# Rows and router of two MoE FFNs in wide pieces kept on chip, the shared expert with stationary weights during the routing

## What is computed

```
x = x + 0.5 * ffn(norm(x))
x = x + attention(norm(x))
x = x + 0.5 * ffn(norm(x))        # the same weights again

ffn(x):  scores = sigmoid(x @ gate_w)                      # 16 experts
         selected = top 2 of scores + expert_bias
         w = scores[selected] / (their sum + 1e-20)
         shared = (silu(x @ sg) * (x @ su)) @ sd           # every token
         routed = sum over the two e: w_e * (silu(x @ g_e) * (x @ u_e)) @ d_e
         return shared + routed                            # hidden width 128
attention(x): per head of 3, per batch of 512 rows:
         S = Q K^T / 16; w = softmax(S, over the queries); w V
         mean over the heads, @ fc_w.T + fc_b
```

## Time and profile before

| | us |
|---|---|
| median of 3 executions | 603.43 |
| lowest and highest | 601.87, 606.74 |
| the profiled execution | 605.9 |
| its span, first to last instruction | 604.7 |
| TensorE busy in it | 478.6 (79%) |
| VectorE busy | 366.6 (61%) |
| ScalarE busy | 274.9 (45%) |
| GpSimd busy | 270.1 (45%) |
| mean granted clock of TensorE | 0.918 of full |

### The profile page before, as it was taken

One profiled execution on the slowest core, in us unless ns is written; L12 is line 12 of the kernel. 1 busy time (PEld: TensorE's weight loads), 2 busy tenths in 40 slices (PEclk: granted clock), 3 DMA queues, 4 the chain that ended last, 5 costly groups with the idle time before them and its releaser, 6 DMA issues.

```text
span 604.7 us, 10587 instructions
## 1 busy us (share of the span) xinstructions
PE 478.6 (79%) x3212; PEld 434.0 (72%) x3212; DVE 366.6 (61%) x1118; ACT 274.9 (45%) x771; POOL 270.1 (45%) x278
## 2 busy tenths in 40 slices
PE   3632389999886799799899988999675899999600
PEld 3632389999774598699879977999563799998500
DVE  5567477566566366557645865543637776766543
ACT  3451147677541444354435443456241277776200
POOL 4654536566042163255226522422203566660675
PEclk9999999999998899899989999999955599999755
DMA  8661134667762010011001100010110156677455
GB/s 277 202 210 34 53 106 150 180 189 147 177 199 70 5 48 2 0 36 54 18 1 41 48 19 2 0 36 1 36 61 10 34 149 177 184 164 177 125 159 142
DMA packets 41077, 56.29 MB, mean 93 GB/s; under 512 B 6272, under 2 KB 33792, under 8 KB 41024
## 3 DMA queue, kind: packets, MB, share of 16 engines
q1 hardware_dynamic: 33024, 34.88, 17.8%
q0 software_dynamic: 7584, 20.72, 15.0%
q10 hardware_dynamic: 416, 0.02, 0.0%
HBM read 36.99 MB, written 18.61 MB: 92 GB/s over the span
## 4 chain that ended last, share of the span: by engine, by line
PE 59%; DVE 14%; DMA 12%; issue 5%; ACT 5%; POOL 5%; SPq 0%; POOLq 0%; ACTq 0%; DVEq 0%
PE bank L299 47%; PE bank L305 6%; DMA stage<-y_dram,slot_i 5%; DMA raw<-xn_dram,gather_at 2%; PE bank L432 2%; DMA raw<-xn_dram 2%; DVE x_sb L991 1%; PE bank L334 1%; POOL stage L1217 1%; DVE softmax_row L1114 1%; POOL w_lo L1167 1%; PE bank L389 1%; DVE x_sb L957 1%; DVE xn L817 1%; DMA xn_dram<-xn 1%
## 5 line engine op out<-in xcount | busy, mean ns | idle before, releaser
L299 PE MATMUL bank<-w_hi,xT 128*128 (+1 forms) x504 | 128.6, 317 | 0.0
L1323 POOL TENSOR_TENSOR e_sp<-raw,e_sp 128x512 fp32r<-128x512 f32 x48 | 62.5, 1302 | 134.7 <-ACT e_sp L773 134.6
L1246 POOL DMA_INDIRECT raw<-xn_dram,gather_at x94 | 89.3, 950 | 57.7 <-PE bank L305 46.8
L299 PEld LDWEIGHTS bank<-w_hi,xT 128*128 128x128 f32 x504 | 92.7, 202 | 0.3
L1217 POOL DMA_INDIRECT stage<-y_dram,slot_i x64 | 61.2, 957 | 51.8 <-issue 26.4
L299 PEld LDWEIGHTS bank<-v_sp,e_sp 128*128 128x128 f32 x576 | 75.8, 194 | 4.0 <-POOL e_sp L1323 1.1
L299 PE MATMUL bank<-v_sp,e_sp 128*128 128x256 f32 x576 | 78.0, 286 | 0.9 <-POOL e_sp L1323 0.9
L299 PE MATMUL bank<-g_sp,xT 128*128 128x512 f32 x288 | 75.2, 396 | 1.4 <-DVE g_sp L1022 1.4
L299 PE MATMUL bank<-w_lo,xT 128*128 (+1 forms) x252 | 74.2, 294 | 0.0
L299 PE MATMUL bank<-w_hi,e_sp 128*128 (+1 forms) x252 | 71.3, 303 | 2.0 <-DVE x_sb L1015 1.8
L305 PE MATMUL bank<-ident,raw 128*128 128x128 f32 x292 | 62.4, 298 | 8.8 <-DMA raw<-xn_dram 5.5
(11 more groups left out here) (112 smaller groups left out, 892.1 us busy)
## 6 DMA issues: line engine op xcount, KB each, us to landing
y_dram<-stage SPq DMA_DIRECT2D x94, 128.0 KB
raw<-xn_dram SPq DMA_DIRECT2D x32, 128.0 KB, 2.3
stage<-in_w_pack SPq DMA_DIRECT2D x9, 384.0 KB, 3.5
raw<-in_w_pack SPq DMA_DIRECT2D x8, 384.0 KB, 3.7
xn_dram<-raw SPq DMA_DIRECT2D x20, 128.0 KB, 1.7
x_sb<-in_x SPq DMA_DIRECT2D x4, 512.0 KB, 5.6
out<-x_sb SPq DMA_DIRECT2D x16, 128.0 KB, 2.3
raw<-xn_dram,gather_at POOLq DMA_INDIRECT x94, 3.4
```

The source lines that it names most:

```text
L299: m = pe.matmul(dst, lhs[k][l], rhs[k][r], start=(first and k == 0 and i == 0), stop=(last and k == n - 1 and i == 2), skip_group_check=True)
L1246: pool.indirect_dma_start(row_buf[:, n % ROWS, :], None, xn_dram, bass.IndirectOffsetOnAxis(ap=gather_at[:, j:j + 1], axis=0)).then_inc(s_ ...
L1323: pool.tensor_tensor(e_sp[:, i, 1, :], e32[:, i, :], e_sp[:, i, 0, :].bitcast(F32), ALU.subtract).then_inc(s_e_lo, 1)
```

## The change

Sizes: `STAGES` is 6 instead of 4 (a new buffer `stage_more`). New buffers lie over memory that is free in that stretch: `xn_all` (all 16 normed tiles) and `x_front` over the fold products, `pick_lane` for all 32 pairs and `pick_tile` over `xn_all`.

1. *Norm in wide pieces.* `front_stats` on VectorE and `front_rstd` on GpSimd measure a batch; ScalarE writes normed rows to `xn_all`; one 512 KB DMA stores a batch. In FFN 2 the first three batches still go through `previous_front` and are reloaded by three DMAs of 512 KB near the end of the attention.
2. *Turned rows stay on chip.* Pairs of tiles are turned into one PSUM bank and split into `front_x`, one buffer of 512 columns a batch, with both parts. The router of FFN 1 and of FFN 2's last batch reads these with `three_pass` against a split gate, six matmuls a tile.
3. *Shared expert with stationary weights.* For a batch, the shared weights are the stationary operand and 512 token columns move: 12 matmuls of 512 columns, one silu, one multiply, one copy and one subtraction of 128x512, then 12 matmuls of 256 columns for Y and two additions to `x_sb`. No shared item is left among the items, which are the 47 slot tiles. In FFN 1 batches 0 to 2 run during the routing and batch 3 after the slot tiles; in FFN 2 all four run during the routing.
4. *Slot index without a ring.* All picks have a buffer. VectorE and GpSimd write lanes, VectorE the tile factors of four tiles at a time with two wide instructions, and TensorE runs all 32 matmuls at one place, behind chunks of eight.
5. *Folds* stand at slot steps 12, 24 and 36, and 3 to 5 behind the slot tiles.

```diff
+    CHUNK = 8
+    EARLY_SHARED = 3
-    STAGES = 4
+    STAGES = 6
+    FOLD_STEPS = (12, 24, 36)
...
+            def front_turn(r, n):
...
+                if n >= 2:
+                    pe.wait_ge(s_pair_lo, r * FRONT_PAIRS + n - 1)
...
+                for q in range(2):
+                    for k in range(KH):
+                        m = pe.transpose(bank[n % 2][:, k * PAIR + q * P:k * PAIR + (q + 1) * P],
+                                         xn_all[:, 2 * n + q, k * P:(k + 1) * P], ident[:])
...
+            def front_router(r, n):
...
+                for q in range(2):
...
+                    m = three_pass(logits_all[:, t * E:(t + 1) * E],
+                                   [[x[:, part, k, cols] for part in range(2)] for k in range(KH)],
+                                   [[gate_sp[:, part, k, :] for part in range(2)] for k in range(KH)])
...
+            def shared_gu(r, b):
...
+                if r == 0 and b >= EARLY_SHARED:
+                    pe.wait_ge(s_hT_lo, NI)
+                    pe.wait_ge(s_y_copy, NI)
+                    pe.wait_ge(s_act, NI)
...
+                if r == 1 and b == 1:
+                    pe.wait_ge(s_mix_add, NT)
+                for half, done in ((0, s_sg), (1, s_su)):
...
+                    three_pass(bank[shared_banks(b)[half]][:], lhs, rhs).then_inc(done, 1)
...
+            def shared_y(r, b):
...
+                pe.wait_ge(s_slo, c + 1)
...
+                    m = three_pass(bank[q // 2][:, q % 2 * H:(q % 2 + 1) * H],
+                                   [[shared_hT[:, part, q * P:(q + 1) * P] for part in range(2)]],
+                                   [[w_hi[:, at:at + H], w_lo[:, at:at + H]]])
...
+            def index_tokens(r):
+                chunks = len(pairs_of) // CHUNK
+                for c in range(chunks):
+                    pe.wait_ge(s_lane_dve, r * DVE_LANES + (c + 1) * DVE_LANES // chunks)
+                    pe.wait_ge(s_lane_pool, r * POOL_LANES + (c + 1) * POOL_LANES // chunks)
+                    pe.wait_ge(s_pick_tile, r * chunks + c + 1)
```

```diff
+            for n in range(FRONT_PAIRS + 1):
+                if n < FRONT_PAIRS:
+                    front_turn(0, n)
+                if n > 0:
+                    front_router(0, n - 1)
+            shared_gu(0, 0)
+            shared_gu(0, 1)
+            rank_tokens(0)
+            shared_y(0, 0)
+            shared_gu(0, 2)
+            pack_experts(0)
+            shared_y(0, 1)
+            index_tokens(0)
+            shared_y(0, 2)
...
+            ffn(0, between1)
+
+            shared_gu(0, 3)
+            fold(next(folded))
+            shared_y(0, 3)
+            for n in folded:
+                fold(n)
...
             for w in MIXED_LATER:
+                if w == U - 1:
+                    front_turn(1, 0)
+                    front_turn(1, 1)
                 mix(w)
...
+            for n in range(2, FRONT_PAIRS - BATCH_PAIRS):
+                front_turn(1, n)
+            shared_gu(1, 0)
+            shared_gu(1, 1)
+            for n in range(FRONT_PAIRS - BATCH_PAIRS, FRONT_PAIRS):
+                front_turn(1, n)
+            for n in range(FRONT_PAIRS - BATCH_PAIRS, FRONT_PAIRS):
+                front_router(1, n)
+            rank_tokens(1)
+            shared_y(1, 0)
+            shared_gu(1, 2)
+            pack_experts(1)
+            shared_y(1, 1)
+            shared_gu(1, 3)
+            index_tokens(1)
+            shared_y(1, 2)
+            shared_y(1, 3)
```

ScalarE and VectorE in FFN 1 from the sigmoid on (`next(r1)` is a piece of `routing`: the last four with picks are the chunks; `run(r1)` ends it with `gather_at`), and VectorE behind the slot tiles:

```diff
+            run(choose(0, 0, NT))
+            shared_silu(0, 0)
+            shared_silu(0, 1)
+            for n in range(4, 8):
+                split_weight(n)
+            shared_hi(0, 0)
+            for n in range(8, 11):
+                split_weight(n)
+            shared_silu(0, 2)
+            shared_hi(0, 1)
+            for n in range(11, 14):
+                split_weight(n)
+            shared_hi(0, 2)
+            for n in range(14, NW):
+                split_weight(n)
...
+            split_weight(2)
+            run(choose(0, 0, NT))
+            shared_mul(0, 0)
+            shared_mul(0, 1)
+            r1 = routing(0)
             next(r1)
             next(r1)
+            shared_lo(0, 0)
+            next(r1)
+            next(r1)
+            next(r1)
+            split_weight(5)
+            next(r1)
+            shared_sink(0, 0)
+            shared_mul(0, 2)
+            next(r1)
+            shared_lo(0, 1)
+            next(r1)
+            split_weight(8)
+            next(r1)
+            shared_sink(0, 1)
+            split_weight(11)
+            shared_lo(0, 2)
+            split_weight(14)
+            shared_sink(0, 2)
+            run(r1)
...
+            shared_mul(0, 3)
+            fold_split(next(folded))
+            shared_lo(0, 3)
+            fold_split(next(folded))
+            shared_sink(0, 3)
             attn_side = [attn_front(b) for b in range(B)]
...
+            next(attn_side[0])
+            fold_split(next(folded))
             run(attn_side[0])
```

GpSimd makes the four `front_rstd`, then splits its weights in order and writes its eight lane picks behind weight 12; the first gather of FFN 1 waits for every weight split and for `gather_at`:

```diff
+                    if r == 0:
+                        pool.wait_ge(s_xn_out, 16 * B)
+                        pool.wait_ge(s_whi, NW)
+                        pool.wait_ge(s_wlo_pool, splits_by(NW - 1, False))
+                        pool.wait_ge(s_wlo_dve, splits_by(NW - 1, True))
...
                     pool.wait_ge(s_indexed, r + 1)
```

More of the change, by code:

```diff
@@ L141, in macaron @@
         g_sp = sbuf("g_sp", [P, 2, KH, N], F32R)
+        with nc.sbuf_tensor("stage_more", [P, 2 * WCOLS], F32) as stage_more:
+            pass
         e_sp = sbuf("e_sp", [P, 2, 2, N], F32R)
@@ L350, in choose, with rank_tokens @@
                     yield
-            def routing(r):
+            def rank_tokens(r):
                 pe.wait_ge(s_choice, 1 + 2 * r)
-                pe.wait_ge(s_front_copy, (r + 1) * NT)
+                if r == 1:
+                    pe.wait_ge(s_g_lo, 2 * B * HEADS)
+                pe.matmul(rank[:, 0:NT, :], before[:], choice[:], start=True, stop=False, skip_group_check=True)
                 for t in range(NT):
-                    pe.matmul(rank[:, t, :], before[:], choice[:, t, :], start=(t == 0), stop=False,
-                              skip_group_check=True)
                     m = pe.matmul(rank[:, t + 1:NT + 1, :], ones[:],
@@ L749, in act_program @@
+            fold_split(next(folded))
+            shared_hi(0, 3)
+            for n in folded:
+                fold_split(n)
+            attn_side = [attn_front(b) for b in range(B)]
             run(attn_side[0])
```

899 lines of the change are left out of this document (432 added, 467 removed).

## The result

The changed kernel is slower: 621.9 us median of 4 runs (616.8 to 624.1), the kernel before 604.0 (4 runs); the ratio is 1.0282, 95% interval 1.0206 to 1.0358. The forecast was 593.7, with a range of 583 to 604. The profiled execution took 621.98 us, span 620.8, against 605.9 and 604.7 before.

A forecast was written before the change was run, and what follows sets the result against it. Bound: TensorE full in slot tiles and attention, GpSimd's gathers in the tail; the change works on stages between. Terms -16.5 +2.1 +1.0 -2.5 +4.6 +0 +2.7 +2.1 -3.3 = -9.8: 605.9 to 596.1 profiled, 593.7 median, range 583 to 604.

The forecast's parts named there:

- T0: First slot tile turned, in FFN 1 at 87.77 us before; forecast at 71.3, a term of -16.5 (bounds -24 to -4).
- Router at 30: Front of FFN 1: the router ends at 30 us, 8 earlier than 37.7, at 0.16 a small matmul.
- Choice: Front of FFN 1: the choice takes 5.9 us without contention and a w_lo split, 9.7 before.
- VectorE's queue: Front of FFN 1: VectorE's work after the rank, up to gather_at, takes 25 us with 2 for waits.
- Contention: Front of FFN 1: six GpSimd splits of w_lo cost VectorE 0.8 us each, +5 (0 to 11).
- C: Rival: in FFN 1 GpSimd's splits and VectorE's routing hold each other up; T0 at 87, 610 us; chance 0.07.
- The 77: Front of FFN 1: T0 nearer 77 us if GpSimd's six splits and VectorE's locking share add up in full.
- Slots: Slot tiles of FFN 1: slow first tiles +2.1 us (0 to 5), three folds inside instead of two +1.0.
- Drain: End of FFN 1's slots: last tile turned to its result takes 4.7 us instead of 7.2, -2.5.
- To the attention: Tile 46's result to first G matmul: 34.2 us instead of 29.6, combines queued behind the last folds; +4.6 (0 to 8).
- Attention: The attention stage: same instructions in the same order, 233.0 us, change 0 (-2 to 2).
- Front of FFN 2: Last mix to first slot tile turned in FFN 2: at 484.5 us instead of 481.77, +2.7 (-5 to 7).

The follow-up runs named there:

- two router runs: Changed kernel with two of three router passes left out (T0 12.2 us earlier), or with 4 small router matmuls a tile instead of 6 in FFN 1 (8.4 earlier).
- early-splits run: Changed kernel with the splits of weights 4 to 10 moved into the router stage; T0 7.6 us earlier, first gather at 77.9.
- hold splits: Changed kernel with GpSimd's split of weight 4 and all after it waiting until VectorE finished the slot arithmetic; T0 moved by 0.7 us.
- combines first: Changed kernel with VectorE combining tiles ahead of the last two fold splits behind FFN 1; first G matmul 29.1 us after tile 46's result.
- router one pass: Changed kernel without two of the three router passes in both FFNs; sigmoid at 27.8 us instead of 39.0, T0 at 76.6.

## Why the prediction was wrong

**T0, the step that failed.** The term was -16.5 and came as +1.0. Two things in it were mis-sized: what a small router matmul costs (0.16, measured 0.213, with TensorE at the lower clock level throughout) and what GpSimd's splits cost VectorE's short operations (+5, measured +11). Its pieces:
- Router at 30, measured 38.8, and the choice began at 39.4 (37.7 before): 9.4 of the miss. I took 0.16 a matmul and let four pairs remain at 20.6; measured 0.213 each, 96 of them 20.4 us, TensorE was behind from 13.7 on, and five and a half pairs remained. I had bounded the small matmul by one of 256 columns and took a value inside the bounds, when it costs as much as that one, the upper end. And I took 30 between 29 for the upper clock level and 34 for the lower, when the stage ran at the lower all through. One row at hand was not used: the plain float32 router took 0.76 a tile, so the new form at 12 x 0.213 a pair, 1.28 a tile, is slower than what it replaces, by 8 us over 16 tiles. The two router runs show that what the router gives back reaches T0 in full (5.6 and 11.2 at the sigmoid, 8.4 and 12.2 at T0). No run kept the plain float32 router in the new kernel.
- Choice, 5.9 forecast: 5.7 measured. Right.
- Rank 2.2 behind the choice, measured 3.1: it stood behind the second shared tile on TensorE, which I had called hidden.
- VectorE's queue, 25 without contention: the early-splits run took 22.5 from the rank to gather_at, and had three splits of 0.95 less in it, so 25.4. Right.
- Contention, +5 forecast: the queue took 35.9 in all (48.2 to 84.1), so 11. I spread 0.8 over each split since VectorE would often be waiting; in fact ScalarE made seven high halves between 46.3 and 53.0, five of them for GpSimd, just when VectorE had its chain of tiny dependent operations. Six tiny operations under five splits lost 6.6 us there, and six picks under five splits 8.1 in hold splits, where 0.8 a split would have been 4: when the operations are short, nearly each of them waits for a whole split.
- First gather at gather_at, T0 3.3 later: 1.5 and 3.3. The copy to the gather I had left out.

So of the rivals C, at 0.07, has the mechanism and, for T0, the number: its gather at 83 to 84 and T0 at 87, measured 85.6 and 88.8 (87.0 in combines first). That its number fits so well is in part luck: its 15.6 for GpSimd's splits came as 11 and its 4 for the router as 9.4, and its weights' chain did not close last (GpSimd's last split ended at 82.1, gather_at was copied at 84.1). Its 610 for the whole was 12 short. What I held against it, that ScalarE's late feeding keeps GpSimd idle between splits, was the error: the late feeding bunched them. The 77 that I worked out for contention taken in full, with the router's 9.4, is 86.

**Slots, +3.1 (2.1 + 1.0):** +3.4 measured, slow first tiles and third fold. Right. **Drain, -2.5:** T46 to tile 46's result took 6.4 (7.2 before), not 4.7. The three last results wait for one another, as the timeline of TensorE at the end of FFN 2 shows:

```profile
570.60 0.38 PE L290 MATMUL bank<-w_hi,e_sp 128*128 x1 [0.44 <-ACT stage L775]
...
571.76 0.38 PE L290 MATMUL bank<-w_hi,e_sp 128*128 x1 [0.36 <-ACT stage L775]
...
573.02 0.38 PE L290 MATMUL bank<-w_hi,e_sp 128*128 x1 [0.65 <-ACT stage L775]
```

Each is 1.2 behind the last, one bank copied out in between. So the end gained 1.7, not 3.3, and the drain of FFN 1 gained 0.8, not 2.5.

**To the attention, +4.6:** from tile 46's result +7.4 (37.0 against 29.6). The mechanism was right (VectorE's queue behind the last fold split) and is shown by combines first. The size held where the clock did: in hold splits and router one pass, whose code is the same from T46 to G, the last split ended 18.6 and 18.7 after the result and G came at 34.2, where I had 19 and 34.2. In the profile after, the last two folds took 3.16 and 3.78 at a granted clock of 0.62 and 0.50; in hold splits 1.99 and 2.49 at 1.00 and 0.77, by the timeline of TensorE in that kernel:

```profile
181.79 1.99 PE L443 MATMUL bank<-route 128*128 128x256 f32 x8
187.47 2.49 PE L443 MATMUL bank<-route 128*128 128x256 f32 x8 [3.69 <-DMA route<-in_fc_t]
```

So 3 us of this part are the clock, which the sum had no term for.

**Attention, 0:** 233.0. Right.

**Front of FFN 2, +2.7:** +6.1 in the profile, and 2.1 to 2.5 in the four faster profiles of the same code. So the size held, and 4 us of the profiled execution are the clock. Two slips in it cancel: the sum from the choice to gather_at leaves out the rank, 2.3 us between the choice and VectorE's first read of it, and the queue behind it took 25.3 instead of 27.5 (combines first: 453.8, 456.1, 481.5). The part had a cheap remedy in view, though: gather_at stood behind sinks that the index does not need, and I counted them in the queue without asking for the order.

The slow first tiles of FFN 2 (+2.1) were +0.8.

## What to carry to other kernels

Matmuls of 16 and of 32 columns with new weights each cost the same here, 0.21 us at the lower clock level (those of 16 columns 0.12 at the upper), so a router split in three passes is three times the time of one pass; count instructions, not columns, and compare with the form that is replaced. When VectorE holds a chain of short dependent operations, look at what GpSimd does in the same microseconds and who feeds it: work that was spread can arrive in a bunch, and each short operation then pays a long one. Before moving work "behind" something, write out the in-order queue of each engine and put first what the next stage waits for; here the order on each engine, ten of the 17 low halves on VectorE instead of five, and eight router matmuls a pair for twelve lay 37 us apart.

## What the hardware showed that I had not expected

- 128x16 and 128x32 router matmuls both 0.21 us apart, with TensorE without a gap for 25 us, and wide matmuls behind them at 0.43 until 44.04, at 0.22 after: the clock was at the lower of its two levels (1.2 and 2.4 GHz) all that time. The PEclk column reads 1.00 for this stretch, so at the start of this trace the spacing of wide matmuls has to be read instead.
- Six lane picks (1.06 us in all when alone) took 9.19 under GpSimd's splits, while two of those splits took 4.28 instead of 3.58: the short operations pay 8.1 us, the long ones 0.7.
- From the last mix on, the clock returns earlier in one profile and later in another over the same instructions: 4 us of 52. Behind FFN 1 it is the same with two folds: 3 us of 37.
